# A two-layer graph network on one core: eight consecutive nodes on a partition instead of two, and another end of the last normalisation

## The reference, cut to what matters

```python
# x: (4096, 128), adj: (4096, 4096), both fp32
def layer0(h, adj):
    filt = tanh(adj * adj) * (adj > 0)
    new_adj = the 350 largest of each row of filt        # a row has some ten entries that are not zero
    h2 = tanh(h @ W_proj + b_proj)
    return relu(new_adj @ (h2 @ W_gcn) + b_gcn)

def layer1(f, adj):
    support = concat([(adj > 0) @ f, (adj < 0) @ f], axis=1)
    node = support @ node_weight + node_bias * diag(adj)[:, None]
    edge = (adj @ f) @ edge_weight + edge_bias * diag(adj)[:, None]
    return node + edge

x = layernorm(x + layer0(x, adj))
x = layernorm(x + layer1(x, adj))
```

## Time and profile before

| | us |
|---|---|
| median of 3 runs | 609.61 (609.23 to 611.47) |
| the profiled execution, its time | 610.62 |
| its span | 608.8 |
| PE busy | 600.5 (99%) |
| DVE busy | 471.2 (77%) |
| ACT busy | 420.4 (69%) |
| POOL busy | 187.7 (31%) |
| DMA | 130.67 MB, mean 215 GB/s |

### The profile page before, as it was taken

The page is one execution under the profiler, slowest core; times in us unless marked ns, Lnnn a source line. Parts: engine busy times, 40 slices in busy tenths (PEclk is TensorE's granted clock), DMA queues, the critical chain, the costliest instruction groups (busy, mean ns, idle before and its releaser), DMA issues.

```text
span 608.8 us, 5805 instructions
## 1 busy us (share of the span) xinstructions
PE 600.5 (99%) x1972; PEld 342.3 (56%) x1972; DVE 471.2 (77%) x690; ACT 420.4 (69%) x315; POOL 187.7 (31%) x88
## 2 busy tenths in 40 slices
PE   9999999999999999999999999999999999999996
PEld 6644444444444444555655656655665665657995
DVE  3767978888797979986497697697697697697843
ACT  3687686868768686558874865965865875865960
POOL 0598798887979697000000000000000000000000
PEclk9999999999999999999999999999999999999999
DMA  8999999999999991049787586586595685775000
GB/s 231 339 340 348 333 332 312 314 280 316 273 340 265 344 208 1 11 128 259 215 240 199 164 249 194 167 234 199 140 270 159 173 240 155 216 197 157 2 17 20
DMA packets 139455, 130.67 MB, mean 215 GB/s; under 512 B 9763, under 2 KB 139430, under 8 KB 139430
## 3 DMA queue, kind: packets, MB, share of 16 engines
q1 hardware_dynamic: 74390, 66.22, 39.3%
q10 hardware_dynamic: 65040, 64.17, 36.7%
HBM read 128.27 MB, written 2.10 MB: 214 GB/s over the span
## 4 chain that ended last, share of the span: by engine, by line
PE 92%; DMA 5%; DVE 1%; POOL 1%; ACT 1%; SPq 0%; issue 0%; DVEq 0%; ACTq 0%
PE acc L1059 34%; PE acc L1045 32%; PE stage L1068 10%; PE stage L1067 10%; DMA a_rows<-in_adj_dram 4%; PE stage L1059 2%; PE to_rows L1074 1%; PE to_rows L1073 1%; PE stage L1007 1%; PE to_rows L1024 1%; DMA x_rows<-in_x_dram 0%; POOL a_cols L390 0%; DVE a_cols L662 0%; ACT a_cols L593 0%; PE stage L1002 0%; POOL a_cols L384 0%
## 5 line engine op out<-in xcount | busy, mean ns | idle before, releaser
L662 DVE STREAM_TRANSPOSE a_cols<-a_rows 128x2048 f32<-128x2048 f32 x120 | 277.2, 2317 | 92.9 <-PE stage L1068 63.4
L1045 PE MATMUL acc<-a_cols,rhs 128*128 128x512 f32 x512 | 221.8, 593 | 1.8 <-ACT a_cols L593 1.1
L1059 PE MATMUL acc<-a_cols,x_rows 128*128 128x512 f32 (+1 forms) x512 | 212.3, 565 | 0.0
L1045 PEld LDWEIGHTS acc<-a_cols,rhs 128*128 128x128 f32 x512 | 96.4, 190 | 121.5 <-issue 117.8
L390 POOL TENSOR_TENSOR a_cols<-a_cols 128x1536 f32<-128x1536 f32 x56 | 153.2, 2747 | 35.0 <-DVE a_cols L662 34.6
L1059 PEld LDWEIGHTS acc<-a_cols,x_rows 128*128 128x128 f32 x512 | 96.6, 190 | 96.3 <-issue 92.4
L611 ACT ACTIVATE a_rows<-a_rows 128x4096 f32<-128x4096 f32 x32 | 116.1, 3627 | 46.2 <-DVE a_cols L662 38.1
L593 ACT ACTIVATE a_cols<-a_cols 128x2048 f32<-128x2048 f32 x56 | 107.1, 1912 | 49.8 <-POOL a_cols L390 49.2
L614 ACT ACTIVATE a_rows<-a_rows 128x4096 f32<-128x4096 f32 x32 | 115.9, 3621 | 1.0
L1067 PE MATMUL stage<-masks,x_hi 128*128 128x512 f32 (+1 forms) x288 | 115.0, 408 | 0.0
L1068 PE MATMUL stage<-masks,x_lo 128*128 128x512 f32 (+1 forms) x288 | 103.0, 366 | 0.0
(11 more groups left out here) (119 smaller groups left out, 271.5 us busy)
## 6 DMA issues: line engine op xcount, KB each, us to landing
a_rows<-in_adj_dram ACTq DMA_DIRECT2D x120, 512.0 KB, 10.4
a_rows<-in_adj_dram SPq DMA_DIRECT2D x120, 512.0 KB, 10.6
out_dram<-n_rows SPq DMA_DIRECT2D x28, 64.0 KB, 7.5
x_rows<-in_x_dram ACTq DMA_DIRECT2D x8, 64.0 KB, 2.5
x_rows<-in_x_dram SPq DMA_DIRECT2D x8, 64.0 KB, 2.4
x_rows<-in_x_dram ACTq DMA_DIRECT2D x4, 128.0 KB, 3.9
x_rows<-in_x_dram SPq DMA_DIRECT2D x4, 128.0 KB, 4.1
diag<-in_adj_dram SPq DMA_DIRECT2D x32, 0.5 KB
```

What stands on the lines that cost most here:

```text
L662: nc.vector.transpose(half_out(hs), half_in(s, h % HALVES)).then_inc(turned[layer], 1)
L1045: last = nc.tensor.matmul(acc[parity][:], rhs[:, b, :], a_cols[:, h % HSLOTS, k, :], start=(b == 0), stop=(b == BLOCKS - 1))
L1059: last = nc.tensor.matmul(sums, x_rows[:, b, :], rows(a_cols[:, h % HSLOTS, k, :]), start=(b == 0), stop=(b == BLOCKS - 1))
```

## The change

1. **Layout.** Partition p of block (s, b) now holds node s*1024 + 8p + b: eight consecutive nodes on one partition. Chunk b is every eighth row of the whole matrix. `half_in` picks the columns accordingly: the read of the 32x32 squares steps over eight elements (32 bytes) where it stepped over two.
2. **Loads and stores.** x comes in five parts, each by one DMA of 64 partitions on each of the two queues, and each run is 2 or 4 KB where it was 1 or 2 KB. The runs of adj remain 1 KB, in DMAs of the same size; neighbouring partitions are now eight rows apart (128 KB; before two rows, 32 KB), and neighbouring runs of a partition 256 rows (4 MB; before 64 rows, 1 MB). The diagonal takes 4 DMAs (before 32), the store of a chunk 1 (before 4), each part of the last store 1 on each queue (before 2).
3. **Reordering copies** become plain ones.
4. **First chunk of layer 1.** Chunk 7 is now the last block of every span, which comes in halves 1, 3, 5 and 7. `norm0(LAST)` runs in one go behind the masks of half 3. PE leaves the last block out of halves 1 and 3, waits for `lo_ready` behind half 3, and does the two left-out blocks then.
5. **Tail.** The root of a quarter of the variance, one step of Heron and a second reciprocal replace the Newton step. In the last part DVE also negates the mean, ACT writes the rows less the mean to `n_rows`, and DVE scales both tiles in one instruction.

```diff
-    X_PARTS = [4, 4, 4, 4, 8, 8]
+    X_PARTS = [4, 4, 8, 8, 8]
+    QUEUE_HALF = [slice(0, P // 2), slice(P // 2, P)]
...
-            return src.rearrange("(r i h) k -> h i r k", h=2, i=SQ)[half]
+            src = adj[:, s * SPAN + q * PCOLS:s * SPAN + (q + 1) * PCOLS]
+            return src.rearrange("(r i b) k -> b i r k", b=PB, i=SQ)[rows]
...
         def half_in(slot, h):
-            return a_rows[:, slot, :, :].rearrange("p r (m j e) -> p e r m j", j=SQ, e=2)[:, h]
+            return a_rows[:, slot, :, :].rearrange("p r (j b) -> p r b j", b=PB)[:, :, h * HB:(h + 1) * HB, :]
...
         def block_of(h, k):
-            return h // HALVES * PB + k * HALVES + h % HALVES
+            return h * HB + k
...
-                for q in SP_QUARTERS:
-                    sp.dma_start(x_of(g, q), x_in(g, q)).then_inc(x_loaded[g], 16)
+                sp.dma_start(x_of(part, 0), x_in(part, 0)).then_inc(x_loaded[part], 16)
...
-                nc.scalar.activation(by_tile(z_t[:]), by_set(acc[parity][:]), ACT.Relu, bias=b_col[:, 1:2])\
+                nc.scalar.activation(z_t[:], acc[parity][:], ACT.Relu, bias=b_col[:, 1:2])\
...
+            act.wait_ge(mean_negated, 1)
+            for k in range(tiles):
+                ins = nc.scalar.activation(n_rows[:, LAST[2], at + k, :], last_rows[1][k], ACT.Identity,
+                                           bias=minus_mean[:, k:k + 1])
+            ins.then_inc(centred, 1)
...
-                for q in ACT_QUARTERS:
-                    act.dma_start(rows_out(rows_of(1, LAST), q)[:, at:at + tiles, :],
-                                  n_rows[SQ * q:SQ * (q + 1), LAST[2], at:at + tiles, :])\
-                        .then_inc(stored[LAST[2]], 16)
+                act.dma_start(rows_out(rows_of(1, LAST))[QUEUE_HALF[1], at:at + tiles, :],
+                              n_rows[QUEUE_HALF[1], LAST[2], at:at + tiles, :]).then_inc(stored[LAST[2]], 16)
...
                     nc.vector.reciprocal(r, root_v[:, 0:tiles]).then_inc(ln_step, 1)
                     waited(ln_step, base + 4)
-                    nc.vector.scalar_tensor_tensor(out=m, in0=r, scalar=-0.5, in1=r, op0=ALU.mult, op1=ALU.mult)\
-                        .then_inc(ln_step, 1)
+                    for k in range(tiles):
+                        ins = nc.vector.scalar_tensor_tensor(out=t[:, k:k + 1], in0=v[:, k:k + 1], scalar=r[:, k:k + 1],
+                                                             in1=root_v[:, k:k + 1], op0=ALU.mult, op1=ALU.add)
+                    ins.then_inc(ln_step, 1)
                     waited(ln_step, base + 5)
-                    nc.vector.tensor_tensor(t, v, m, ALU.mult).then_inc(ln_step, 1)
-                    waited(ln_step, base + 6)
-                    nc.vector.scalar_tensor_tensor(out=r, in0=t, scalar=1.5, in1=r, op0=ALU.add, op1=ALU.mult)\
-                        .then_inc(ln_step, LN_STEPS - 6)
+                    nc.vector.reciprocal(r, t).then_inc(ln_step, LN_STEPS - 5)
...
+                    if root_of:
+                        at = PARTS[root_of][0]
+                        rows = n_rows[:, LAST[2], at:at + tiles, :]
+                        waited(centred, 1)
+                        nc.vector.tensor_tensor(rows, rows, r.unsqueeze(2).broadcast_to([P, tiles, F]), ALU.mult)\
+                            .then_inc(normed, 1)
+                        return
...
                     if not before:
-                        if h in (3, 4, 5):
-                            norm0(LAST, h - 3)
+                        if h == HSLOTS - 1:
+                            for part in range(3):
+                                norm0(LAST, part)
...
-                for h in range(HPC):
-                    if h == 0:
-                        pe.wait_ge(lo_ready, CHUNKS - 1)
-                    if h == HPC - HALVES:
-                        pe.wait_ge(lo_ready, CHUNKS)
+                waiting = [h for h in range(HSLOTS) if h % HALVES]
+                pe.wait_ge(lo_ready, CHUNKS - 1)
+                for h in range(HSLOTS):
                     pe.wait_ge(masked, h + 1)
-                    with_adj(acc[0][:], h, all_rows)
+                    ready = range(HB - 1) if h in waiting else range(HB)
+                    with_adj(acc[0][:], h, all_rows, ready)
...
+                pe.wait_ge(lo_ready, CHUNKS)
+                for h in waiting:
+                    with_adj(acc[0][:], h, all_rows, [HB - 1])
+                    with_masks(acc_m[0][:], h, all_rows, [HB - 1]).then_inc(half_used[1], 1 if h == 1 else 2)
+                for h in range(HSLOTS, HPC):
+                    pe.wait_ge(masked, h + 1)
+                    with_adj(acc[0][:], h, all_rows)
+                    with_masks(acc_m[0][:], h, all_rows).then_inc(half_used[1], 1)
```

More of the change, by code:

```diff
@@ L114, in build @@
         eps = sb("eps", [P, 1])
+        minus_mean = sb("minus_mean", [P, TILES])
         y2 = sb("y2", [P, TILES])
@@ L189, in rows_at, with diag_at @@
         def rows_at(t, rows):
[L190 to L201, removed]
+            return t.rearrange("p (s b) f -> p b s f", b=PB)[:, rows]
+        def diag_at(rows, s):
+            return diag[:, s * PB + rows:s * PB + rows + 1]
         def part_of(cols, at, tiles):
-            return cols.rearrange("p (q m i) -> p q m i", q=QUARTERS, i=SQ)[:, :, at:at + tiles, :]\
-                .rearrange("p q m i -> p q (m i)")
+            return cols[:, at * P:(at + tiles) * P]
         feat_t = early[:, 0, :]
@@ L312, in rows_of @@
         def rows_of(layer, chunk):
-            return (chunk[1] * -1 + (PIECES - 1), 1 - chunk[2]) if layer else (chunk[1], chunk[2])
+            return CHUNKS - 1 - chunk[0] if layer else chunk[0]
         def next_of(chunk):
-            c, span, parity = chunk
-            return c + 1, span + parity, 1 - parity
+            return chunk[0] + 1, None, 1 - chunk[2]
         def is_first(c):
@@ L434, in _ @@
                 for span in range(PIECES):
[L435 to L440, removed]
+                    sp.dma_start(diag[:, span * PB:(span + 1) * PB],
+                                 bass.AP(adj.tensor, span * SPAN * (N + 1), [[PB * (N + 1), P], [N + 1, PB]]))\
+                        .then_inc(wl1_loaded, 16)
             def store(chunk):
@@ L445, in store @@
                 sp.wait_ge(normed, CHUNKS + c + 1)
-                for q in range(QUARTERS):
-                    sp.dma_start(rows_out(rows, q),
-                                 n_rows[SQ * q:SQ * (q + 1), parity, :, :]).then_inc(stored[parity], 16)
+                sp.dma_start(rows_out(rows), n_rows[:, parity, :, :]).then_inc(stored[parity], 16)
             def layer1(chunk, before):
@@ L1054, in all_rows, with with_adj @@
                 return cols
-            def with_adj(sums, h, rows):
-                for k in range(HB):
+            def with_adj(sums, h, rows, part=range(HB)):
+                for k in part:
                     b = block_of(h, k)
@@ L1061, in with_adj, with with_masks @@
                 return last
-            def with_masks(sums_m, h, rows):
-                for k in range(HB):
+            def with_masks(sums_m, h, rows, part=range(HB)):
+                for k in part:
                     b = block_of(h, k)
```

102 lines of the change are left out of this document (48 added, 54 removed).

## The result

The changed kernel takes 720.03 us in the median of 6 runs (715.09 to 725.7) against 609.68 (609.23 to 611.47): a ratio of 1.181, 95% interval 1.1755 to 1.1865. The forecast was 607.2. The profiled execution took 715.09 us, its span is 713.3.

The account below looks back on a forecast made before the run. PE was taken as the bound, busy 600.5 of 608.8 us. Head 1.7 plus tail 0.7 gave 2.4 us won, all else 0, so the median 609.61 becomes 607.2; range 605.8 to 610.6.

Parts of the forecast that it names:

- The transposes: DVE's large turns: expected to stay at 2317 ns each despite the 32-byte read step, cost 0; upper end twice as long.
- rival 1: The wide read step slows DVE's turns: about 642 us at 3.5 us a turn, 766 at 4.6; chance 0.11.
- The pitch of adj: Loads of adj: the wider spacing of runs in HBM was expected to leave the 344 GB/s rate unchanged.
- Where layer 1 begins: Layer 1's first chunk, reordered: `lo_ready` 7.5 us before PE needs it, cost 0, at most 1 us.
- Head: Before layer 0 and the second chunk: earlier loads and fewer issues shorten PE's waits, 1.7 us won (0 to 2.0).
- The saving of issues: Head queues: 7 fewer issues of x at 0.45 us each, 3.2 us less, first adj loads at about 3.8 us.
- the piece of the second chunk: Head: the late last quarter of adj for the second chunk lands 1 to 3 us earlier, likeliest 2.
- Rival 3: Only the tail is won; the second chunk's piece stays late because queues are full either way: 608.9 us, chance 0.13.
- Tail: After PE's last product: root step, scaling and stores together win 0.7 us (0.3 to 0.9).
- Scaling: Tail: one DVE operation on 256 columns takes 0.41 us where two took 0.72, 0.31 won.
- Heron's step: Tail: Heron's step and a second reciprocal in place of Newton's step let scaling begin 0.12 us earlier.
- Stores: Tail: one issue of each pair goes, 0.35 us won less at most 0.2 for twice the bytes; counted as 0.3.

Follow-up runs that it names:

- experiment 1: The changed kernel with the turns reading every second element (8 bytes) as before, all else of the change kept: 610.63 us against 610.3, ratio 1.0012.
- experiment 2: The kernel before with only the turns' read step widened to every eighth element (32 bytes): 718.86 us, ratio 1.1766.
- experiment 3: The kernel before with half h of each chunk turned at a read step of h + 1 elements (4 to 32 bytes): one run, 658.67 us.
- experiment 4: The kernel before with odd halves copied at steps of 1, 2, 4, 8 elements, and some POOL and ACT accesses stepped by 8: one run, 645.26 us.
- experiment 6: The kernel before with the change's ACT centring and single scaling, and ACT's five head loads of adj issued with groups 0 to 4: 610.39 us, ratio 1.0000.
- experiment 7: The changed kernel with the narrow read, x in six parts, and 32-partition DMAs for x and the last stores: 610.4 us, ratio 1.0006.

## Why the prediction was wrong

**The transposes.** This is the step that failed, as the prediction put it: "one element at a time is slow enough that I expect no change: 0". The runs showed 3.94 us for 2.32 at the step of 32 bytes, by the read alone (experiments 1 to 4). The mechanism was rival 1's, and at 3.94 us, which is over both of its points of decision (2.9 in layer 0, 3.5 in layer 1), both layers are DVE's. The time of 720 lies between its two estimates, 642 for 3.5 us and 766 for 4.6. Its working with the measured 3.94 gives 7 x 8.4 = 59 and 7 x 3.6 = 25 us, 84 in all, where 104.5 were measured. In layer 0 the seven chunks from the second on grew by 55.5 us, near the 59. The first chunk, which I left out, added 8.4 (the second began at 61.23 instead of 52.85); there the small turns are slower too:

```profile
L656 DVE STREAM_TRANSPOSE a_cols<-a_rows 128x1024 f32<-128x1024 f32 x16 | 31.2, 2005 | 0.0
```

Before, they took 1215 ns. In layer 1, six chunks in its middle grew by 28.1 us, 4.7 each where the working has 3.6; what comes before them added 4.7 and the last chunk with the tail 7.9. PE's clock, which was at its lower level behind some long waits, may be a part of this; how much wasn't measured.

What was wrong with the reasoning is that the nearest row was taken as evidence though it lay on the other side of the very thing that changed. A row with two elements in each 16-byte line says nothing about one with a single element. The sentence that I drew from the Trainium skill (SBUF — State Buffer, the note on SBUF cachelines) puts a step of eight elements on the slow side, and there the trace agrees: 3.94 us for 2.32. With nothing measured against it and 1.6 us of DVE at stake 120 times, its chance of 0.11 was too low.

**The pitch of adj.** Right: 344 and 301 GB/s at the new pitch, once DVE is not in the way (experiment 1).

**Where layer 1 begins.** Right as far as it goes, and in its parts: with narrow turns PE is busy 44.00 of 44 us from 249 on, cost 0. `x1_lo` is written at 260.21 and PE comes to it at 267.72, 7.5 us of cover as forecast, and DVE turns half 5 from 269.24 on, forecast 269.6 (layer 1 begins 0.8 us earlier in this profile than in that of the kernel before). In the changed kernel itself the cover isn't there, since DVE is late by then.

**Head.** Mis-sized: 1.7 us forecast, at most 0.73 seen in experiment 1, which is no more than the unchanged head varies by, and no gain in the medians. The first term failed, "everything in the head before that is PE's own chain, which the change leaves alone": a merged load of x lands later, PE started its second group 1 us late, and layer 0 began at 24.12 where I forecast 23.1. The saving of issues was too large as well, since a merged issue of x takes 0.56 us or more and not 0.45: ACT's first load of adj left at 4.73, not 3.8. And the piece of the second chunk, put at 2 us earlier, came 0.77 earlier (45.65 to 44.88), within the variation again. Rival 3, that a piece is late because the queues are full either way, fits what experiments 6 and 7 show; it isn't shown by itself.

**Tail.** Forecast 0.7. Scaling: 0.31 forecast, 0.30 measured. Heron's step: 0.12 forecast, none measured; from ACT's root to the scaling it is 1.19 us (603.58 to 604.77) against 1.20 (604.28 to 605.48), because the two single-column operations take 0.35 together. Stores: 0.3 forecast, a loss measured: from the end of the scaling to the end of the span there are 3.0 us in experiment 1 and 2.6 before. I allowed 0.2 for twice the bytes; from issue to landing it took 0.6 more, and the one issue (0.67) nearly as long as the two (0.76). No second table load appeared.

## What to carry to other kernels

Before the step of an access on a busy engine is widened, look at how many elements it leaves in each 16 bytes: here one instead of two made the same instruction 1.7 times as long, and the few microseconds to be won elsewhere could not pay for it. If no row of the profile has the new pattern, measure the one instruction by itself before arguing from the nearest one. A merged DMA is waited for as a whole: here PE's second group of the head started 1 us later for it. And before a gain of under a microsecond is read from one profile, look at how much the unchanged part differs between profiles: this head's second chunk varied by 1.3 us with nothing changed in it.

## What the runs showed of the hardware that was not expected

- DVE, fp32, 2048 elements on 128 partitions: turn 2.3 us at steps of 4 and 8 bytes, 3.9 to 4.1 at 16 to 32 bytes; copy 1.22 at 4 and 8 bytes, 2.20 at 16 and 2.05 at 32. ACT in place, from a plain pass to a step of 32 bytes in reading and writing: 3.62 to 7.98 us (4096 elements). POOL in place, likewise: 2.75 to 3.04 us (1536 elements), the least affected.
- From 2 to 13 us the DMAs moved 243 to 259 GB/s in the mean, and 343 or 344 from 24 to 57 us, in the kernel before and in experiments 1, 6 and 7 alike, whatever was issued when. The cause stays open.
- In experiment 4 the copies also depend on what else runs. Those in layer 0, where POOL squares beside them, took 2.05 to 4.19 us (18 of them, between 100 and 235 us), those in layer 1, where POOL is idle, 1.22 to 2.31; the turns took 2.3 to 2.4 us in both. The timeline of DVE and POOL shows why, first for a copy with a step of 2 elements and then for one with a step of 4:

```profile
115.26 2.92 DVE L685 COPY a_cols<-a_rows 128x2048 f32<-128x2048 f32 x1 [2.50 <-PE acc L1070]
117.05 3.73 POOL L410 TENSOR_TENSOR a_cols<-a_cols 128x1536 f32<-128x1536 f32 x1
...
123.45 2.74 POOL L410 TENSOR_TENSOR a_cols<-a_cols 128x1536 f32<-128x1536 f32 x1
124.06 4.19 DVE L685 COPY a_cols<-a_rows 128x2048 f32<-128x2048 f32 x1
```

The second copy ends at 128.25, 2.06 us after POOL's square ended at 126.19, which is about the time that such a copy takes alone. The first ends at 118.18, 1.1 us after the square before it, and POOL's next square, which began at 117.05, lasts 3.73 us where others last 2.74. So a copy and a square of POOL took turns here, each waiting for the other, at narrow and wide steps alike; a turn went on beside the squares (2.31 us at 106.27, with a square from 106.43 on).
